# A two-layer decoder on one core: twelve norms and one split go from VectorE and GpSimd to ScalarE, and all engine lists are ordered anew

## The reference

```python
def _layernorm(x, axis=-1, eps=1e-05):
    m = jnp.mean(x, axis=axis, keepdims=True)
    v = jnp.var(x, axis=axis, keepdims=True)
    return (x - m) / jnp.sqrt(v + eps)

x = x + _L0_attn_ref(_layernorm(x), Wqkv, Wo)            # 16 heads, rope, causal
x = x + _L0_xattn_ref(_layernorm(x), ctx_2048)           # x @ ctx[b].T, both rounded to fp8 in blocks
x = x + _L0_ffn_ref(_layernorm(x), Wg, W1, W3, W2, ...)  # 16 experts of 176, top 4 in 2 groups, and a shared one
x = x + _L1_attn_ref(_layernorm(x), w_qkv, w_proj)       # int8 rows, ternary weights, causal
x = x + _L1_xattn_ref(_layernorm(x), tok, ctx, ctx, ctx) # expert e = token id // 3125: silu(g) * u, down
x = x + _L1_ffn_ref(_layernorm(x), w_gate, w_up, w_down) # int8 rows, ternary weights, 1024 inner
```

## Time and profile before

| | us |
|---|---|
| median of 3 runs | 551.89 |
| runs | 552.65, 551.89, 547.5 |
| the profiled execution, its own time | 550.15 |
| its span, first to last instruction | 548.4 |
| TensorE busy | 505.2 |
| VectorE busy | 418.2 |
| ScalarE busy | 332.5 |
| GpSimd busy | 190.7 |

### The profile page before, as it was taken

The page is one execution under the profiler, slowest core; times in us unless marked ns, Lnnn a source line. Parts: engine busy times, 40 slices in busy tenths (PEclk is TensorE's granted clock), DMA queues, the critical chain, the costliest instruction groups (busy, mean ns, idle before and its releaser), DMA issues.

```text
span 548.4 us, 11908 instructions
## 1 busy us (share of the span) xinstructions
PE 505.2 (92%) x4768; PEld 370.6 (68%) x4768; DVE 418.2 (76%) x941; ACT 332.5 (61%) x576; POOL 190.7 (35%) x262
## 2 busy tenths in 40 slices
PE   6888878788999999999999998999999999999975
PEld 5443533455877887778788777868787666577744
DVE  3889897698747999557996878664778478688884
ACT  3357645656676236893366763678455963866686
POOL 3709477843121035220022714222036301126352
PEclk9899898998999999999999999999999999999989
DMA  8043244120000002000000100200001100000001
GB/s 293 19 180 100 90 155 139 61 71 8 1 1 4 1 1 78 1 2 1 2 3 1 54 25 1 79 1 1 1 1 57 62 1 1 3 0 1 20 21 38
DMA packets 5942, 21.66 MB, mean 39 GB/s; under 512 B 896, under 2 KB 3072, under 8 KB 5120
## 3 DMA queue, kind: packets, MB, share of 16 engines
q1 hardware_dynamic: 5888, 20.91, 11.1%
HBM read 19.86 MB, written 1.05 MB: 38 GB/s over the span
## 4 chain that ended last, share of the span: by engine, by line
PE 60%; DVE 25%; ACT 8%; issue 4%; POOL 2%; ACTq 0%; DVEq 0%; POOLq 0%
PE ps L1050 21%; PE ps L1084 14%; DVE nmx L2468 5%; PE ps L800 2%; DVE y L2375 2%; PE ps L929 2%; PE ps L822 2%; DVE hl L2586 2%; PE ps L853 2%; PE ps L858 2%; PE ps L1060 2%; PE ps L784 2%; PE ps L1130 1%; PE ps L906 1%; DVE hs L2575 1%
## 5 line engine op out<-in xcount | busy, mean ns | idle before, releaser
L2575 DVE TENSOR_TENSOR hs<-hs,ps 128x512 f32<-128x512 f32 (+1 forms) x68 | 45.0, 666 | 35.0 <-PE ps L1050 17.9
L1910 ACT ACTIVATE hs<-ps 128x512 f32<-128x512 f32 (+1 forms) x68 | 39.2, 581 | 43.9 <-PE ps L1050 39.9
L2468 DVE TENSOR_REDUCE nmx<-ps 128x2 f32<-128x512 f32 (+1 forms) x96 | 60.7, 680 | 6.0 <-PE ps L858 5.8
L1917 ACT ACTIVATE hh<-hs 128x512 f16<-128x512 f32 (+1 forms) x52 | 31.6, 610 | 41.6 <-DVE hs L2581 26.8
L544 POOL TENSOR_TENSOR ve<-mv,half 128x2 f32<-128x2 f32 x24 | 6.0, 251 | 144.7 <-DVE mv L2362 144.7
L1084 PE MATMUL ps<-w2h,hh 128*128 128x256 f16 x200 | 54.9, 275 | 0.1
L1084 PE MATMUL ps<-w2l,hh 128*128 128x256 f16 x200 | 54.8, 274 | 0.0
L1084 PE MATMUL ps<-w2h,hl 128*128 128x256 f16 x200 | 54.7, 273 | 0.0
L2586 DVE TENSOR_TENSOR hl<-hs,hh 128x512 f16<-128x512 f32 (+1 forms) x52 | 37.8, 736 | 6.3 <-ACT hh L1917 6.1
L2581 DVE TENSOR_TENSOR hs<-hs,ps 128x512 f32<-128x512 f32 (+1 forms) x52 | 34.5, 663 | 9.6 <-PE ps L1060 8.6
L1050 PE MATMUL ps<-yah,w1h 128*128 128x256 f16 x200 | 38.8, 276 | 2.1 <-DVE hs L2575 2.0
(11 more groups left out here) (247 smaller groups left out, 1354.7 us busy)
## 6 DMA issues: line engine op xcount, KB each, us to landing
stage<-in_w SPq DMA_DIRECT2D x12, 800.0 KB, 4.2
tstage<-in_tern SPq DMA_DIRECT2D x4, 1024.0 KB, 4.9
cs<-in_ctxT SPq DMA_DIRECT2D x1, 1024.0 KB, 9.4
cd<-in_ctxT SPq DMA_DIRECT2D x1, 1024.0 KB, 4.7
out_x<-xs SPq DMA_DIRECT2D x4, 256.0 KB, 2.2
sels<-in_sel SPq DMA_DIRECT2D x1, 800.0 KB, 9.5
w0s<-in_w SPq DMA_DIRECT2D x1, 768.0 KB, 6.7
xs<-in_x SPq DMA_DIRECT2D x1, 768.0 KB, 8.0
```

The costliest lines, as they stand in the source:

```text
L1910: act.activation(hs[:, n % 3, 0:w], ps[:, gate_bank(n), 0:w], ACT.Silu).then_inc(e_sil.sem, 1)
L1917: act.activation(hh[:, n % 2, 0:w], hs[:, n % 3, 0:w], ACT.Copy).then_inc(e_hi.sem, 1)
L2468: dve.tensor_reduce(nmx[:, int(n % 3 > 0), first + par:first + 2 * heads:2], ps[:, max_bank(it, n) + par, :].rearrange("p (h k) -> p h k", ...
L2575: TT(hs[:, n % 3, 0:w], hs[:, n % 3, 0:w], ps[:, up_bank(n), 0:w], ALU.mult).then_inc(e_hb.sem, 1)
```

## The change

Twelve norms, those that only TensorE reads, are computed by ScalarE as x * rstd + (-mean * rstd). The shift comes from GpSimd: two small instructions more for each, `nsh` = -mean before `rstd`, and `nmr` = nsh * rstd after it. The eight other norms (context and ffn) and the four heads of the second attention stay on VectorE. The high half `ch` of the context is now made by ScalarE in one instruction, the low half `cl` by GpSimd in four pieces of 128x512, and stands behind the first piece of the mixture's weights. The first transposes and the masks wait for the constants alone, no longer for the small identity `id16`, which has a semaphore of its own. The five lists are ordered anew throughout; TensorE's fillers at the start go from 33, 17 and 22 to 8, 19 and 12, and those of `awake` from 144 to 130 in all.

```diff
+        def by_scalar(kind, b):
+            return kind in ("router", "tail") or kind == "head" and b < B
...
                 g.tensor_tensor(ve[:, ln % 2, :], mv[:, ln % 2, :, 1], half[:, 8:10], ALU.add).then_inc(veps.sem, 1)
                 g.wait_ge(veps.sem, ln + 1)
+                older = [key for key in ln_turn if ln_turn[key] == ln - 2 and by_scalar(*key)]
+                if older:
+                    g.wait_ge(ya_ok.sem, ya_turn[older[0]] + 1)
+                if by_scalar(kind, b):
+                    g.tensor_tensor(nsh[:, ln % 2, :], mv[:, ln % 2, :, 0], half[:, 2:4], ALU.mult)
                 g.tensor_tensor(rstd[:, ln % 2, :], ve[:, ln % 2, :], half[:, 0:2], ALU.pow).then_inc(rstd_ok.sem, 1)
+                if by_scalar(kind, b):
+                    g.wait_ge(rstd_ok.sem, ln + 1)
+                    g.tensor_tensor(nmr[:, ln % 2, :], nsh[:, ln % 2, :], rstd[:, ln % 2, :], ALU.mult).then_inc(shift_ok.sem, 1)
...
             def context_split():
-                g.wait_ge(d_ctx.sem, 16)
-                g.tensor_scalar(ch[:, :, :, :], cs[:, :, :, :], 1.0, None, ALU.mult).then_inc(c_hi.sem, 1)
                 g.wait_ge(c_hi.sem, 1)
-                g.tensor_tensor(cl[:, :, :, :], cs[:, :, :, :], ch[:, :, :, :], ALU.subtract).then_inc(c_lo.sem, 1)
+                for b in range(B):
+                    last = g.tensor_tensor(cl[:, b, :, :], cs[:, b, :, :], ch[:, b, :, :], ALU.subtract)
+                last.then_inc(c_lo.sem, 1)
...
+            def context_high():
+                act.wait_ge(d_ctx.sem, 16)
+                act.activation(ch[:, :, :, :], cs[:, :, :, :], ACT.Copy).then_inc(c_hi.sem, 1)
+
+            def normed(kind, b):
+
+                ln = ln_turn[kind, b]
+                dst = y if kind == "head" else yr
+                act.wait_ge(shift_ok.sem, ya_turn[kind, b] + 1)
+                if kind == "head" and b == 1:
+                    act.wait_ge(fT.sem, f_turn["head", 0] + 1)
+                elif kind == "head" and b:
+                    act.wait_ge(q_ok.sem, b - 1)
+                elif kind != "head" and (kind, b) != ("router", 0):
+                    act.wait_ge(fT.sem, f_turn[(kind, b - 1) if b else ("router", B - 1)] + 1)
+                for j in range(JT):
+                    last = act.activation(dst[:, j, :], xs[:, 2 * (b % B) + j, :], ACT.Identity,
+                                          scale=rstd[:, ln % 2, j:j + 1], bias=nmr[:, ln % 2, j:j + 1])
+                last.then_inc(ya_ok.sem, 1)
...
-            awake_first(1, 33)
+            awake_first(1, 8)
             first_turn(0)
-            awake_first(1, 17)
+            awake_first(1, 19)
             project(0, 0)
-            awake_first(1, 22)
+            awake_first(1, 12)
             project(0, 1)
```

More of the change, by code:

```diff
@@ L392, in decoder @@
         y_ok = sig("y_ok")
+        ya_ok = sig("ya_ok")
+        shift_ok = sig("shift_ok")
         x_ok = sig("x_ok")
@@ L482, in decoder @@
         ln_turn = {key: n for n, key in enumerate(order)}
+        def by_scalar(kind, b):
+            return kind in ("router", "tail") or kind == "head" and b < B
+        ya_turn = {key: n for n, key in enumerate([key for key in order if by_scalar(*key)])}
+        y_turn = {key: n for n, key in enumerate([key for key in order if not by_scalar(*key)])}
         order = [("head", 0)]
@@ L754, in _ @@
             products(5, 0)
+            products(5, 1)
             inverse_root(5)
-            products(5, 1)
             products(6, 0)
@@ L809, in stack @@
             def stack(it, u):
+                if it == 0 and u == 0:
+                    pe.wait_ge(d_id.sem, 16)
                 if u == 0:
@@ L1551, in _ @@
-            pe.wait_ge(o_ok.sem, 10)
+            scores_max(5, 3)
+            up(36)
+            back(4, 1)
+            spread(36)
+            scores_max(5, 4)
+            down(33)
+            gate(37)
+            up(37)
+            scores_max(5, 5)
+            spread(37)
+            down(34)
             router_turned(4)
-            gate(37)
-            scores_max(5, 5)
-            up(37)
-            spread(37)
+            gate(38)
+            rounded_output_turned(4)
+            up(38)
@@ L1589, in _ @@
-            project(6, 0)
-            gate(43)
-            back(5, 0)
-            spread(42)
-            project(6, 1)
-            down(40)
-            up(43)
+            up(43)
+            project(6, 0)
+            back(5, 0)
+            gate(44)
+            project(6, 1)
+            spread(43)
+            scores_exp(5, 5)
             down(41)
-            spread(43)
-            gate(44)
+            down(42)
+            values(5, 2)
             up(44)
+            spread(44)
@@ L1662, in _ @@
             scores_exp(6, 5)
-            back(6, 0)
             project(7, 1)
-            gate(55)
             down(53)
@@ L2001, in _ @@
             slices(6)
-            slices(7)
-            quantised('context', 0)
             exponentials(1, 0)
             exponentials(1, 1)
+            slices(7)
+            slices(8)
             exponentials(1, 2)
+            quantised('context', 0)
+            normed('head', 2)
+            first_turn(2)
+            normed('router', 0)
             exponentials(1, 3)
-            first_turn(2)
-            slices(8)
+            experts_hi('moe', 0, 0)
             slices(9)
-            experts_hi('moe', 0, 0)
-            slices(10)
             stacks(2, 0)
@@ L2134, in _ @@
             silu_of(28)
+            magnitudes(1)
+            quantised('context', 3)
+            silu_of(29)
             exponentials(4, 0)
+            rounded_rows('head', 5)
+            inner_high(28)
             exponentials(4, 1)
-            inner_high(28)
-            exponentials(4, 2)
-            silu_of(29)
-            rounded_rows('head', 5)
             inner_high(29)
             first_turn(5)
+            exponentials(4, 2)
             silu_of(30)
+            stacks(5, 0)
```

1120 lines of the change are left out of this document (559 added, 561 removed).

## The result

| | before | change |
|---|---|---|
| median, us | 549.69 (4 runs, 546.94 to 552.65) | 534.54 (4 runs, 533.55 to 535.2) |
| ratio | | 0.9722, interval 0.9656 to 0.9788 |
| span of the profiled execution | 548.4 | 532.4 |
| its own time | 550.15 | 534.2 |
| busy TensorE, VectorE, ScalarE, GpSimd | 505.2, 418.2, 332.5, 190.7 | 493.6, 396.9, 345.2, 190.4 |

The change is 15.2 us faster; the prediction said 9.1. (The kernel before now stood 2.2 lower than in the runs that the prediction started from; 9.1 less would have been 540.6 here.

The account below looks back on a forecast made before the run. TensorE's own work was taken to bound 121 to 516 us, and a chain of waits the start. Terms 5.0 + 1.8 + 1.0 + 1.0 + 0.3 = 9.1 us less gave 542.8 from 551.89; range 537 to 549.5.

Parts of the forecast that it names:

- the start: First 60 us, up to the transposes of queries and keys: 5.0 us less, transposes at 23.7; bounds 2.5 and 5.5 less.
- the collision: Before 30 us: GpSimd's long `ch` and `cl` block VectorE's `rr` and `y` through shared ports, on the chain of waits.
- Part b: Batch 2's head, 85 to 92 us: norm ahead of GpSimd's weights piece, transposes then await context's addition; 1.8 us less.
- a: The kernel's start, up to the transposes of queries and keys: 5.0 us less.
- Part c: Ahead of the first expert product: `yTl` behind all maxima 0.6 less, router 0's norm 0.4 less; bounds 0 and 1.4.
- Part d: Mixed part, from the first expert product: eight norms leave VectorE, new list order; 1.0 less, bounds 5 less, 4 more.
- Part e: Last 32.6 us: no norm moves, seven fillers go; 0.3 us less, bounds 1.5 less and 2 more.
- That the head moves the end one to one: What lies ahead of 121 us moves the end equally, as long as the first expert product can start earlier.
- Weights holding the start of the experts: Last weights piece, split just ahead of the first expert product, limits its gain to 2.4, not 7.8: 548.2; chance 0.15.
- The collision moves: `cl`'s pieces at about 40 us collide with VectorE's context scaling; gain only 3.8, so 548.1; chance 0.12.
- New waits on ScalarE: Norms in ScalarE's list hold up exponentials and `silu`, then TensorE; at 1.6 us each of ten norms, 558.8; chance 0.07.
- The new order helps the mixed part more: Mixed part, from the first expert product: reordered lists save 5 us more than forecast, 538.8; chance 0.10.

## Why the prediction was wrong

**The sign and the mechanism of the start were right.** No `y` or `rr` over 1 us before 30 us; the granted clock at full level in the first 20 us; transposes of queries and keys at 24.38 against the 23.7 worked out, 4.3 in place of **5.0**. With the new lists the collision is worth about that to the end: 4.5 by undoing the split, though it then stands 5 us later than in the kernel before. With the old ones it is worth 2.9.

**Part b** said that the transposes of batch 2 wait for the context's addition once the norm is out of the way. They do. But the addition ends only 2.2 us earlier than before (88.04 against 90.25): I had carried the 5.0 of the start through to it, and the context's chain, with the collision of `c` and `ve` in it, passed on about half of the 4.3. The transposes come 4.0 earlier, where a and b together said 6.8. **Part c** said 1.0; from those transposes to the first expert product it is 1.8 shorter (27.15 against 28.92). The product comes at 115.25, 5.7 earlier, where the sum said 7.8 and 113.2. Up to here the forecast was 2.1 too large.

**Part d is the failed step**: "I take **1.0** less." Its windows ran to the last `down`, and that stretch lost 8.7 (393.76 to 385.08), beyond the bound of 5. The sentence that this part "can give back 11.2 us at most" took all busy time as work. TensorE's idle time there did fall, from 11.2 to 7.0; beside it 2.7 us of fillers went, and some 1.7 us of half clock, two terms that the sum didn't have (some 0.6 of the 8.7 is work that now stands behind the cut). That the order of the lists does most of it is shown: 4.4 less with no norm moved for the part up to the maxima of iteration 7, and some of the end's gain lies ahead of the last `down` as well.

**Part e failed in the same way, by less**: "No norm moves there; seven fillers go ... **0.3** less, bounds 1.5 less and 2 more." Its stretch lost 1.6, or 2.2 with the moved work. I read it as a chain of fixed length and gave the order no price, though the earlier trace rows show TensorE idle for 8.7 us of it. Nor do the seven fillers go there: 15 became 14, and the other six went ahead of the last `down`. Taken as the experiments cut it, from the maxima of iteration 7 on, the end lost 5.3 by the windows; its order alone is worth 4.0 on the kernel before and 6.2 on the change.

**That the head moves the end one to one** is a sentence that the other lists decide. It is true behind the new order (2.7 for 2.7, 4.4 for 4.5). Behind the old one, of 6.5 at the first product 1.7 are left in the median, and these aren't clear of noise.

**The rivals.** Weights holding the start of the experts: wrong, the last piece is split at 113.80, the first expert product starts at 115.25 and the chain ahead of it runs over TensorE and ScalarE. The collision moves: with the pieces at 41 us and at 21 us it does, and doesn't cost the gain; a collision that no rival named, `c` and `ve` at 72 us, delays the context's chain by some 2 us. New waits on ScalarE: in the old order the kernel with all moves is slower, on average 1.0 for each norm; in the new order norms on ScalarE gain instead. The condition of this rival wasn't the norms but the places of the norms. The new order helps the mixed part more, by 5 us (538.8): the nearest, and right in kind, but still too small. The range left this side out at 537. Bounds of 5 for part d and 1.5 for part e, both taken, gave 537.6, so it is the bound of part d, 5 against 8.7, that the time fell through; the 2.1 by which the start was forecast too large hid part of that.

What isn't settled: which engine's order makes the gain of the end, which calls make that of the mixed part, and what the new order of the head is worth without the norms, which no run has with the old order behind it.

## What to carry to other kernels

When engines run lists written out by hand, a change that moves work and orders the lists anew is two changes, and the second can be the larger one: here the order with no norm moved was worth some 8 of 15 us (4.4 in the mixed part, 4.0 in the end), and the moves without the order cost 7. Give the order a price wherever TensorE waits in the profile before, the end included. Fillers and a granted clock under 1.00 stand in busy time, and both can come back. And don't count on a gain ahead of a mixed part to reach the end: here it did behind one order of the lists and not behind the other.

## What the runs showed that I had not expected

A norm of 128x256 on ScalarE with scale and shift as columns takes 584 to 612 ns for each half, against 407 for VectorE's `y` and 500 for ScalarE's `qf` with a scale alone: I had taken 500. A collision of VectorE and GpSimd shifts to whatever VectorE does then: 2.97 for an `rr` of 0.69 and 3.94 for a `qst` of 0.42 in one kernel, and with GpSimd's work in pieces, which took 1.2 to 1.6 each, 1.1 to 1.4 for each of four. GpSimd's reduction over partitions stands in the trace with 0.39 us, and its next instruction comes 7.2 us behind it ("7.22 <-issue" at 37.61): a busy time that doesn't show the price.
